# Four column strips for every whole-array matmul of two self-attention stages

## The reference

```python
# layer 0 (16 heads of 8): causal softmax, and cross attention to 64 context tokens
att = jnp.einsum('bhqd,bhkd->bhqk', q, k) * scale
att = jnp.where(causal[None, None], att, -jnp.inf)
y = jnp.einsum('bhqk,bhkd->bhqd', jax.nn.softmax(att, axis=-1), v)
...
y = y + jnp.einsum('bhqk,bhkd->bhqd', jax.nn.softmax(attc, axis=-1), vc)
return y.transpose(0, 2, 1, 3).reshape(x.shape[0], T, C) @ Wp + bp

# layer 1, first attention (16 heads of 32): softmax over all keys, then the mask
a = jax.nn.softmax(jnp.einsum('bhsd,bhtd->bhst', q, k) * D ** (-0.5), axis=-1)
a = a * (jnp.arange(t)[None, :] > jnp.arange(s)[:, None])
o = jnp.einsum('bhst,bhtd->bhsd', a, v)
x_out = x + o @ li1_w + li1_b
```

## Time and profile before

| what | us |
|---|---|
| median of 3 runs (lowest, highest) | 1775.41 (1774.73, 1778.52) |
| the profiled execution, its own time | 1778.97 |
| its span, first to last instruction | 1777.2 |
| TensorE busy in it | 1463.7 |
| VectorE, ScalarE, GpSimd busy | 1008.6, 790.3, 733.9 |

### The profile page before, as it was taken

One profiled execution on the slowest core, in us unless ns is written; L12 is line 12 of the kernel. 1 busy time (PEld: TensorE's weight loads), 2 busy tenths in 40 slices (PEclk: granted clock), 3 DMA queues, 4 the chain that ended last, 5 costly groups with the idle time before them and its releaser, 6 DMA issues. The chain is left out here.

```text
span 1777.2 us, 44907 instructions
## 1 busy us (share of the span) xinstructions
PE 1463.7 (82%) x16109; PEld 1005.8 (57%) x16110; DVE 1008.6 (57%) x2501; ACT 790.3 (44%) x2349; POOL 733.9 (41%) x1243
## 2 busy tenths in 40 slices
PE   4899999999977779999999968689999978813870
PEld 2465656565555545666666645457777765613870
DVE  3465656565536756665666537757777757630431
ACT  1445454545442235555555523156666643301430
POOL 4233333333314637777777756601111104333006
PEclk9899999999988989999999989879999999955995
DMA  3340000000001200000000002200000013201115
GB/s 95 108 108 20 12 21 14 18 15 11 11 20 48 83 22 17 20 11 20 20 20 8 14 23 75 62 13 25 23 19 27 18 31 101 71 27 45 55 54 134
DMA packets 129397, 68.47 MB, mean 39 GB/s; under 512 B 20312, under 2 KB 125356, under 8 KB 129212
## 3 DMA queue, kind: packets, MB, share of 16 engines
q1 hardware_dynamic: 127164, 61.75, 12.4%
q0 software_dynamic: 2048, 4.20, 0.9%
HBM read 41.80 MB, written 24.12 MB: 37 GB/s over the span
## 5 line engine op out<-in xcount | busy, mean ns | idle before, releaser
L1070 ACT ACTIVATE space<-scores 128x512 f32<-128x512 f32 x576 | 315.3, 550 | 359.5 <-PE scores L917 291.7
L1156 DVE TENSOR_REDUCE space<-scores 128x2 f32<-128x512 f32 (+1 forms) x512 | 305.7, 622 | 253.2 <-PE scores L917 173.5
L888 PE MATMUL scores<-space 32*128 32x256 f32 (+1 forms) x2304 | 197.6, 412 | 26.4 <-DVE space L1156 16.7
L430 ACT ACTIVATE space<-scores,space 128x64 f32<-128x64 f32 x512 | 152.9, 328 | 89.7 <-DVE space L600 89.7
L1289 POOL TENSOR_SCALAR_AFFINE_SELECT space<-space 128x512 f32<-128x512 f32 x128 | 81.7, 638 | 264.7 <-ACT space L1070 264.7
L1301 POOL TENSOR_TENSOR space<-space 128x1024 f32<-128x1024 f32 x64 | 150.8, 2356 | 0.0
L917 PE MATMUL scores<-space 32*128 32x256 f32 (+1 forms) x2048 | 149.7, 359 | 0.0
L888 PEld LDWEIGHTS scores<-space 32*128 32x128 f32 x2304 | 94.0, 188 | 87.6 <-DVE space L1156 34.6
L1518 ACT ACTIVATE space<-scores,w_later_cols 128x512 f32<-128x512 f32 x96 | 65.7, 687 | 124.9 <-PE scores L1467 123.1
L1293 POOL TENSOR_SCALAR_AFFINE_SELECT space<-space 128x512 f32<-128x512 f32 x128 | 81.6, 638 | 85.3 <-ACT space L1070 85.3
L430 ACT ACTIVATION_READ_ACCUMULATOR space<-scores,space 128x1 f32 x512 | 112.3, 220 | 0.0
(11 more groups left out here) (301 smaller groups left out, 3279.2 us busy)
## 6 DMA issues: line engine op xcount, KB each, us to landing
space<-in_x SPq DMA_DIRECT2D x32, 128.0 KB, 2.2
x<-space SPq DMA_DIRECT2D x16, 256.0 KB, 3.2
space<-xx SPq DMA_DIRECT2D x32, 128.0 KB, 2.2
xo<-space SPq DMA_DIRECT2D x32, 128.0 KB, 1.8
space<-xo SPq DMA_DIRECT2D x16, 256.0 KB, 2.9
space<-xm SPq DMA_DIRECT2D x32, 128.0 KB, 2.1
space<-x SPq DMA_DIRECT2D x16, 256.0 KB, 3.7
sorted_in<-zeros SPq DMA_DIRECT2D x10, 256.0 KB
```

What stands on the lines that cost most here:

```text
L430: last = act.activation(k.pc[:, c % 2, h * TC:(h + 1) * TC], k.scores[0][:, at:at + TC], ACT.Exp, bias=k.cmax[:, c % 2, h:h + 1], scale=1. ...
L888: last = pe.matmul(a.score_bank(j)[:, 0:n], q[rows, e * P:(e + 1) * P], keys[rows, 0:n], start=not cut, stop=True, skip_group_check=True)
L1070: act.activation(pt[:, 2 * pair:2 * pair + 2, lo:S], a.score_banks(pair)[:, :, S + lo:2 * S], ACT.Exp, bias=0.0, scale=1.0)\
L1156: last = dve.tensor_reduce(out[:, c % 2, 2 * pair:2 * pair + 2], banks[:, :, 0:n], AX.X, ALU.max, negate=True)
```

## The change

A helper `strips` replaces a whole-array matmul by four, each with 32 of its stationary columns and the same moving data, into 32 partitions of the same bank. It is used for the mask matmul of the first stage and for all pieces that took the whole array. Transposes become matmuls with the identity as moving data: the f32 ones thereby turn from one instruction a block into two in each of four strips. `low` goes, the bf16 maxima arrive as f32 in PSUM, and the copy to bf16 (now L1209) reads f32. The three 64-row matmuls, the 32-row ones and the values stay. No order, no wait and no buffer changes.

```diff
+    def strips(out, left, right, start=True, stop=True):
+        for j in range(4):
+            part = slice(32 * j, 32 * j + 32)
+            last = pe.matmul(out[part], left[:, part], right, start=start, stop=stop, skip_group_check=True)
+        return last
...
             for j in range(4):
-                pe.matmul(a.score_bank(j)[:, e * P:n], k.identb[:, :], k.above[:, :], start=True, stop=False, skip_group_check=True)
+                strips(a.score_bank(j)[:, e * P:n], k.identb[:, :], k.above[:, :], True, False)
...
         if kind == a.T:
-                last = pe.transpose(bank[:, blk * P:(blk + 1) * P], k.wn[:, b % 2, blk], k.ident[:, :])
+                last = strips(bank[:, blk * P:(blk + 1) * P], k.wn[:, b % 2, blk], k.ident[:, :])
...
         if kind == a.Q:
-            last = pe.matmul(bank[:, 0:S], w["wq"][:, n * P:(n + 1) * P], k.xq[:, b % 2], start=True, stop=True)
+            last = strips(bank[:, 0:S], w["wq"][:, n * P:(n + 1) * P], k.xq[:, b % 2])
...
         if kind == a.N:
-                last = pe.transpose(a.low(bank)[:, blk * P:(blk + 1) * P], k.nmax3[:, part % 2, blk], k.identb[:, :])
+                last = strips(bank[:, blk * P:(blk + 1) * P], k.nmax3[:, part % 2, blk], k.identb[:, :])
         if kind == a.U:
-                last = pe.transpose(bank[:, blk * P:(blk + 1) * P], k.den[:, blk * P:(blk + 1) * P], k.ident[:, :])
+                last = strips(bank[:, blk * P:(blk + 1) * P], k.den[:, blk * P:(blk + 1) * P], k.ident[:, :])
         if kind == a.R:
-                    last = pe.transpose(bank[:, g * S + blk * P:g * S + (blk + 1) * P], k.rx[:, blk, at:at + P], k.ident[:, :])
+                    last = strips(bank[:, g * S + blk * P:g * S + (blk + 1) * P], k.rx[:, blk, at:at + P], k.ident[:, :])
...
-            dve.tensor_copy(a.maxima(a.part_end(part) - 1), a.low(bank)[:, 0:S]).then_inc(s["max_ready"].sem, 1)
+            dve.tensor_copy(a.maxima(a.part_end(part) - 1), bank[:, 0:S]).then_inc(s["max_ready"].sem, 1)
```

More of the change, by code:

```diff
@@ L1000, in piece @@
             wait(pe, s["side"], b + 1)
-            last = pe.matmul(bank[:, 0:S], w["wq"][:, n * P:(n + 1) * P], k.xq[:, b % 2], start=True, stop=True)
+            last = strips(bank[:, 0:S], w["wq"][:, n * P:(n + 1) * P], k.xq[:, b % 2])
             if a.G == 4:
-                last = pe.matmul(bank[:, S:2 * S], w["wk"][:, n * P:(n + 1) * P], k.xk[:, b % 2], start=True, stop=True)
+                last = strips(bank[:, S:2 * S], w["wk"][:, n * P:(n + 1) * P], k.xk[:, b % 2])
             else:
-                last = pe.matmul(bank[:, S:2 * S], w["wcq"][:, :], k.xq[:, b % 2], start=True, stop=True)
+                last = strips(bank[:, S:2 * S], w["wcq"][:, :], k.xq[:, b % 2])
             last.then_inc(s["q_full"].sem, 1)
         if kind == a.K:
-            pe.matmul(bank[:, 0:S], w["wk"][:, :], k.xq[:, b % 2], start=True, stop=True)
+            strips(bank[:, 0:S], w["wk"][:, :], k.xq[:, b % 2])
             pe.matmul(bank[:, S:S + TC], w["wck"][:, :], k.xc[:, b % 2, 0], start=True, stop=True).then_inc(s["k_full"].sem, 1)
@@ L1012, in piece @@
             if a.G == 4:
-                last = pe.matmul(bank[:, :], x[:, b % 2, n * P:(n + 1) * P], w["wv"][:, :], start=True, stop=True)
+                last = strips(bank[:, :], x[:, b % 2, n * P:(n + 1) * P], w["wv"][:, :])
             else:
                 for blk in range(SB):
-                    pe.matmul(bank[:, blk * P:(blk + 1) * P], x[:, b % 2, blk * P:(blk + 1) * P], w["wv"][:, :], start=True, stop=True)
+                    strips(bank[:, blk * P:(blk + 1) * P], x[:, b % 2, blk * P:(blk + 1) * P], w["wv"][:, :])
                 last = pe.matmul(bank[:, S:S + P], k.xc[:, b % 2].rearrange("c h t -> c (h t)"), w["wcv"][:, :], start=True, stop=True)
@@ L1041, in piece @@
                 for g in range(groups):
-                    last = pe.matmul(bank[:, o * P:(o + 1) * P], k.ot[:, g, blk * P:(blk + 1) * P], w["wo"][:, g if a.G == 4 else 0],
-                                     start=(g == 0), stop=(g == groups - 1))
+                    last = strips(bank[:, o * P:(o + 1) * P], k.ot[:, g, blk * P:(blk + 1) * P], w["wo"][:, g if a.G == 4 else 0],
+                                  g == 0, g == groups - 1)
             last.then_inc(s["y_full"].sem, 1)
```

2 lines of the change are left out of this document (removed).

## The result

| what | before | after |
|---|---|---|
| median us (lowest, highest), 7 runs each | 1776.21 (1774.73, 1780.79) | 1784.84 (1781.83, 1786.8) |
| the profiled execution, its own time | 1778.97 | 1785.86 |
| its span | 1777.2 | 1784.1 |

The measured ratio of all runs is 1.004, with a 95% interval from 1.0026 to 1.0053 (the two medians alone give 1.0049): slower, by more than the 0.2% that the prediction called no change. The forecast was 1780.5, range 1772 to 1791, with 0.54 for slower. The profiled execution came out 6.9 us longer where 5.1 were forecast.

A forecast was written before the change was run, and what follows sets the result against it. TensorE or VectorE's reduces, differing by slot, were taken to bound the kernel. Per batch +0.58 us (first stage) and -0.24 (second), over 15 batches 8.7 - 3.6 = +5.1 us: profiled execution 1784.1, median 1780.5, range 1772 to 1791.

The forecast's parts named there:

- Transposes double: Both stages: f32 transposes take two passes instead of one; slots +0.28 and +0.31 us in the first, +0.24 each in two of the second.
- Drains and first loads go between equal shapes: Both stages, slots TensorE sets: neighbours of one shape need no drain or first load, e.g. -0.17 us first stage, -0.20 second.
- Slots set by the reduces keep their time: Slots whose window starts 0.10 us after VectorE's reduces end: what TensorE saves there goes to the wait, no gain.
- array-only rival: Both stages: waits move with TensorE and all its savings count; -7.4 us, 1768, faster; chance 0.07.
- bf16 strips overlap: First-stage mask: sixteen bf16 instructions run in four rounds of 0.055 us, as long as before the change.
- The rival with 1807 or 1858: First-stage mask: bf16 strips overlap badly (+26 us, 1807) or not at all (+78 us, 1858); chance 0.10.
- Waiting windows 0.05 dearer each: First stage, four windows a batch that start from a wait: each ends 0.05 us later, +0.20 a batch.
- the rival that called it zero: First stage: windows that start from a wait cost nothing more; total +2.1 us, 1777.5, no change; chance 0.20.
- the first stage's forecast of +8.7: First stage, ten slots a batch: +0.58 us a batch over 15 batches, 8.7 us longer.
- The second stage: Second stage, eight slots a batch without mask matmul: -0.24 us a batch over 15 batches, 3.6 us shorter.

## Why the prediction was right, and where it was not

- **Transposes double.** Right: R +0.28 in the first stage (1.32 forecast, 1.31 read) and +0.24 twice in the second, N and U +0.33 for +0.31. The run with T, U and R whole, 1.0% faster than the changed kernel, shows that they carry the loss.
- **Drains and first loads go between equal shapes.** Right: N and Q -0.16 for -0.17, Q with V -0.20 for -0.20, the two Y slots -0.22 and -0.21 for -0.22, Q alone -0.10 for -0.08. The two runs with V, Y and Q in strips cash it in.
- **Slots set by the reduces keep their time.** Right, and it is what separates the forecast from the array-only rival: T, K and the plain slots moved by 0.02 at most, and the window starts stay 0.11 behind VectorE. Y gave 0.05, V 0.05 where I had passed its saving on.
- **bf16 strips overlap.** Right: 0.33 a mask. The rival with 1807 or 1858 fell. The Trainium skill's rule that column tiling has no fast weight load (TensorEngine Tiling (Array Packing), Restrictions) cost nothing that shows here: sixteen loads take 0.26.
- **Waiting windows 0.05 dearer each.** The step that was mis-sized: the price is about 0.02. From load to the next line's load, before and after, behind a wait:

```profile
310.43 0.24 PEld L885 LDWEIGHTS scores<-above,identb 128*128 128x128 bf16 x4
310.77 0.31 PEld L888 LDWEIGHTS scores<-space 32*128 32x128 f32 x8
```

```profile
315.58 0.26 PEld L872 LDWEIGHTS scores<-above,identb 128*32 128x32 bf16 x16 [0.29 <-DVE space L1159]
315.95 0.20 PEld L891 LDWEIGHTS scores<-space 32*128 32x128 f32 x4
```

  0.343 became 0.367 (to three digits; the rows round). I had put the skew of the four strips (0.02) and 0.03 more for loads that come after a wait. Only the first is there: the 0.34 beside 0.31 of the earlier trace rows is spent either way. By the slots, those windows cost 0.06 a batch together, not 0.20, and the first-stage batch rose by 0.42, not 0.58: 15 x 0.16 = 2.4 us less than forecast. The size was wrong and the rival that called it zero was nearer, at that step.
- **A term that was not in the sum.** The pauses in the instruction stream, +2.3 us, nearly the same size: the first stage's forecast of +8.7 met +8.6 for a partly wrong reason. Nothing in the trace of before showed them, and no row there could have priced them; what was in reach was the count, half as many instructions again in the first stage, most of them where each has little array time.
- **The second stage** came to -0.20 a batch for -0.24; N with U, and N with T, are +0.02 and +0.03 where I had 0. Its first batch lost 1.7 to the clock, and what lies outside the two stages gained 0.9, which no step had.
- **The total.** That the forecast of +5.1 lies near the measured +6.9 is partly luck. The terms that it was made of come to +3.2 (6.3 - 3.1), between its own 5.1 and the 2.1 of the rival without dearer windows, and below the 3.6 us that it called no change. The rest are pauses and clock, which it did not have.

On that clock the runs say one thing more. The run with only the mask in strips has the second stage's instructions of the kernel before, word for word, and its first batch (the same eight windows) took 21.65 us for 19.81:

```profile
637.60:647.60 10.00, 8.59 (x39) 4.65 (x36) 4.12 (x7) 1.90 (x5) 0.00 (x0) 0.58 0.00 0
```

The granted clock is 0.58, as in the changed kernel. Of the traces of this study only those of the kernel before and of the run with V, Y and Q in strips have the high one:

```profile
628.30:638.30 10.00, 8.18 (x96) 3.10 (x96) 5.63 (x9) 2.49 (x6) 0.93 (x4) 0.90 0.01 2
```

So this is no cost of the strips in that stage. Nor does TensorE's work in the ten us ahead tell the two apart: 3.9 and 3.7 us busy in the two traces with the high clock, 3.9 in this one and 3.6 to 4.1 in the others. What decides between the two in a given program or execution was not tested and stays open; in a single pair of traces it is worth 1.7 us, a third of what was forecast. Behind the second stage, where all programs are the same, the traces differ by up to 3.4 us. Open, too, is how long a pause will be: at the same record, 2241, it was 0.84 in one program and 1.15 in another, and at most records of that kind none shows. Why a packet comes late at one place and not at another was not tested.

## What to carry to other kernels

Count three things for an edit of tiling: what the array streams (an f32 transpose by `transpose` is one pass, by a matmul with the identity two), what the change of shape takes at each border (here 0.10 to drain, and up to 0.11 more where a first f32 load of 128 columns stands open), and how many instructions stand in how little array time. Convert the pieces whose neighbours already have the new shape and whose slot TensorE sets, and leave the others: all in strips was 0.4% slower, the chosen ones 0.9% faster. A term that is right in total is not yet right in its parts; the stages and slots have to be compared one by one.

## What the hardware showed that I had not expected

- TensorE's instructions come in packets of 256 (16.4 KB), and at one fixed place in every 256 TensorE can stand for 0.1 to 1.47 us. The six long ones set beside the packets end 1.3 to 1.7 us after one has landed. Moving the code by 32 instructions freed the nine windows that had paused and left one large and two small pauses elsewhere.
- Sixteen bf16 strips of 128 columns keep the pace of four whole matmuls, 0.33 to 0.34 for a mask with its drain. Thirty-two strips of 64 columns, the same columns, take 0.39 behind other strips.
- The start of the second stage had a granted clock of 0.57 to 0.60 or of 0.85 to 0.90, in one case for the same instructions (0.58 and 0.85), with 21.35 to 21.65 or 19.2 to 19.8 us for its first batch.
